# Attention probabilities times values behind the interleaved jobs instead of ahead of them, in a gated cross-attention and feed-forward kernel

## The reference

```
q = rope((layernorm(x) @ Wq) per head)            # 32 heads of 16
k = rope((ctx @ Wk) per head);  v = ctx @ Wv
w = softmax(q k^T / 4)                            # per batch and head, 256 x 256
x = x + tanh(g_xattn) * ((w v) @ Wout + bout)
h = square(relu(layernorm(x) @ up)) @ down + (layernorm(x) @ expert) * (sum of the 2 largest gate logits)
x = x + tanh(g_ffn) * (layernorm(h) * gamma + beta)
```

## Time and profile before

| | |
|---|---|
| median of 3 runs | 1567.08 us |
| the profiled execution | 1566.75 us, span 1564.9 us |
| TensorE, matmul busy | 1515.9 us (97% of the span) |
| TensorE, weight load busy | 1125.0 us (72%) |
| VectorE busy | 980.2 us (63%) |
| ScalarE busy | 635.0 us (41%) |
| GpSimd busy | 337.9 us (22%) |
| chain that ended last | TensorE 88%, VectorE 7%, issue 2% |
| mean granted TensorE clock | 0.986 of full speed |

### The profile page before, as it was taken

One profiled execution on the slowest core, in us unless ns is written; L12 is line 12 of the kernel. 1 busy time (PEld: TensorE's weight loads), 2 busy tenths in 40 slices (PEclk: granted clock), 3 DMA queues, 4 the chain that ended last, 5 costly groups with the idle time before them and its releaser, 6 DMA issues.

```text
span 1564.9 us, 25920 instructions
## 1 busy us (share of the span) xinstructions
PE 1515.9 (97%) x9498; PEld 1125.0 (72%) x9498; DVE 980.2 (63%) x1416; ACT 635.0 (41%) x962; POOL 337.9 (22%) x406
## 2 busy tenths in 40 slices
PE   7789999999999999979999999999999999999997
PEld 6556666666666666646787888878888888788886
DVE  7788888888888888755655436435354264453524
ACT  4365665655555666665432222222222222222221
POOL 5323233333333333112101002001020020110202
PEclk9699999999999999999999999999999999999999
DMA  6645555555555555544411001101011010010101
GB/s 174 142 98 141 134 137 138 131 142 139 135 135 143 127 127 136 121 134 120 147 61 35 27 21 47 35 15 47 21 35 47 1 54 27 22 40 21 55 0 41
DMA packets 80623, 131.11 MB, mean 84 GB/s; under 512 B 21624, under 2 KB 35064, under 8 KB 80504
## 3 DMA queue, kind: packets, MB, share of 16 engines
q1 hardware_dynamic: 80504, 129.48, 32.4%
HBM read 51.17 MB, written 16.78 MB: 43 GB/s over the span
## 4 chain that ended last, share of the span: by engine, by line
PE 88%; DVE 7%; issue 2%; POOL 1%; ACT 1%; DMA 0%; SPq 0%; POOLq 0%; DVEq 0%; ACTq 0%
PE pP L1113 17%; PE pT L1113 11%; PE pA L1314 11%; PE pO L1113 11%; PE pB L1314 11%; PE pA L1211 7%; PE pO L1239 7%; PE pB L1227 3%; PE pM L1113 3%; DVE mneg L1534 3%; PE pP L1120 2%; PE pM L1120 2%; PE pT L1195 1%; PE pM L1281 1%; PE pM L1187 1%
## 5 line engine op out<-in xcount | busy, mean ns | idle before, releaser
L1534 DVE TENSOR_REDUCE mneg<-pA 128x4 f32<-128x1024 f32 x250 | 305.7, 1223 | 97.7 <-PE pA L1211 93.2
L1012 ACT ACTIVATE probs<-pB 128x1024 f32<-128x1024 f32 x249 | 255.8, 1027 | 213.2 <-PE pB L1227 203.3
L811 POOL TENSOR_SCALAR var_eps<-meanvar 128x1 f32<-128x1 f32 x96 | 34.6, 360 | 986.1 <-DVE meanvar L1416 985.9
L1637 DVE TENSOR_TENSOR relu<-relu 128x512 f32<-128x512 f32 x128 | 88.4, 690 | 252.3 <-ACT hid L1066 252.3
L1314 PE MATMUL pA<-dn,hid 128*128 128x512 f32 x768 | 197.1, 392 | 1.7 <-DVE hid L1639 1.5
L1314 PE MATMUL pB<-dn,hid 128*128 128x512 f32 x768 | 195.0, 389 | 0.0
L1113 PE MATMUL pP<-fT,up 128*128 128x512 f32 x768 | 188.5, 394 | 0.0
L1113 PE MATMUL pO<-fT,up 128*128 128x512 f32 x768 | 184.7, 389 | 0.0
L1314 PEld LDWEIGHTS pA<-dn,hid 128*128 128x128 f32 x768 | 142.9, 188 | 34.4 <-DVE hid L1639 5.1
L1113 PEld LDWEIGHTS pO<-fT,up 128*128 128x128 f32 x768 | 144.0, 188 | 30.3 <-issue 0.4
L1314 PEld LDWEIGHTS pB<-dn,hid 128*128 128x128 f32 x768 | 144.1, 188 | 30.0
(11 more groups left out here) (200 smaller groups left out, 1989.8 us busy)
## 6 DMA issues: line engine op xcount, KB each, us to landing
stk<-kT SPq DMA_DIRECT2D x180, 128.0 KB, 2.9
stq<-qT SPq DMA_DIRECT2D x180, 128.0 KB, 2.9
fres<-x_scratch SPq DMA_DIRECT2D x34, 256.0 KB, 2.9
xin<-x SPq DMA_DIRECT2D x32, 256.0 KB, 2.9
numer<-av_s SPq DMA_DIRECT2D x128, 64.0 KB, 2.4
xres<-x SPq DMA_DIRECT2D x32, 256.0 KB, 2.9
x_scratch<-xres SPq DMA_DIRECT2D x32, 256.0 KB, 2.4
out<-y_s SPq DMA_DIRECT2D x32, 256.0 KB, 2.0
```

Of the source, the lines that this page charges most:

```text
L811: nc.gpsimd.tensor_scalar_add(var_eps[:], meanvar[:, 1:2], EPS).then_inc(ve_made, 1)
L1012: nc.scalar.activation(probs[:, s % 4, :, :, :].rearrange("p a b s -> p a (b s)"), psum[:, :, :], ACT.Exp).then_inc(exp_done, 1)
L1534: nc.vector.tensor_reduce(mneg[par][:, :, 2 * u:2 * u + 2].rearrange("p t q -> p q t"), psum[:, :, :].rearrange("p q (t k) -> p q t k", t= ...
L1637: nc.vector.tensor_tensor(r[:], r[:], r[:], ALU.mult).then_inc(sq_made, 1)
```

## The change

In TensorE's step, the loop over the jobs moves ahead of the product:

```diff
@@ -1260,12 +1260,12 @@
                     if within(i):
                         logits_b(i, par % 2, s)
+                    for name in names_at(i, s):
+                        job(name, i, par)
                     if s in VALUES and within(i):
                         times_v(i, par % 2, VALUES[s])
                     elif s == 0 and within(i - 1):
                         times_v(i - 1, (par + 1) % 2, GROUPS - 1)
-                    for name in names_at(i, s):
-                        job(name, i, par)
                     if planned(tile_at, i, s) is not None:
                         turned(0, planned(tile_at, i, s))
```

## The result

| | us | ratio to before, 95% interval |
|---|---|---|
| before, median of 4 runs beside it | 1567.06 | |
| changed, median of 4 runs (1586.88 to 1589.35) | 1587.12 | 1.013 [1.0113, 1.0148] |
| changed, profiled execution | 1586.89, span 1585.1 | |

The change costs 20.1 us. The forecast was 1586, from 1580 to 1594. All of it arises in the attention loop: the kT1 of iteration 13 starts at 653.93 instead of 633.92, 20.0 us late, and the first matmuls of the feed-forward gate (L1281) start at 748.37 instead of 728.02, 20.35 us late, against 20.2 us in the span.

The account below looks back on a forecast made before the run. It took TensorE's stream in the attention loop as the limit, busy 41.91 of 42.06 us an iteration. Losses of 13.7 us at step 9 and 5.5 at steps 5 to 7 gave 1586, range 1580 to 1594.

Parts of the forecast that it names:

- The work on TensorE: Attention loop: same matmuls with new neighbours leave no hole, 0 us, with 0.01 us either way for each of 7 steps.
- Step 9: kT1 loses the product that covered its wait for GpSimd's sum: 0.98 us in each of 14 iterations, 13.7 us.
- Steps 5 to 7: ScalarE stands at pO, so step 6's exp and b(7) come late: 0.39 us, 14 times, 5.5 us.
- The sum: Whole kernel: 13.7 + 5.5 = 19.2 us more, 1586.3 us against the median of 1567.08.
- The other steps: Steps 0, 10, 12, 14: ScalarE's lateness covered by six-matmul jobs, 0 us; X0 in step 0 pays 0 to 0.02 us.
- Only step 9: Rival: only step 9 is paid, ScalarE's pile-up in step 6 finds slack; 1580.8 us, chance 0.16.
- More jobs late: Rival: X0, X1, V0 or b(14) also arrive ahead of their input, 3 to 8 us; 1589 to 1594, chance 0.13.
- The clock: Rival: TensorE's waits of about 1.1 us lower its clock, 1.7 us an iteration, 24 us; 1610, chance 0.05.
- Cheaper neighbours: Rival: product beside logits is cheaper, so each of 7 steps gains; 12 us faster, 1555, chance 0.03.
- No change: Rival: waits at kT1 and b(7) are absorbed because the rotation chain comes earlier; 1567, chance 0.03.

Follow-up runs that it names:

- e8: Changed kernel, with K1's and Q1's rotations ahead of maxima(8) and maxima(9), and step 5's pO copy behind those of kT0 and X1: 1566.13 us, ratio 0.9996.
- e1: Kernel before, with the new order (jobs, then product) in step 9 alone: 1581.39 us, ratio 1.0097.
- e2: Kernel before, with the new order (jobs, then product) in step 5 alone: 1572.53 us, ratio 1.0037.
- e5: Changed kernel, with ScalarE's copy of step 5's pO put behind the copies of kT0 and X1: 1581.75 us, ratio 1.0106.
- e3: Kernel before, with the new order in steps 0, 2, 10, 12 and 14 only: 1572.66 us, ratio 1.0038.
- e4: Changed kernel, with K1's two rotation products ahead of maxima(8) on VectorE: 1579.16 us, ratio 1.0081.
- e9: Kernel before, old order, with K1's rotation ahead of maxima(8), kT0 moved from step 5 to 6, K1 using pT: 1564.05 us, ratio 0.9984.

## Why the prediction was right, point by point

**The work on TensorE: 0.** Right, and shown twice: steps 0, 2, 12 and 14 keep their length to within 0.02 us in the changed kernel, in the median of the iterations (for instance step 14, 3.25 before and 3.26 after), and e8 has the new order at no cost. The Trainium skill ("TensorEngine Tiling (Array Packing)", Key Properties) has a drain at each change of mode; the runs agree in that the same number of changes costs the same, in whichever order; what one change costs, none of them shows alone.

**Step 9, 0.98 us.** Right to the hundredth: the step takes 3.31 us where it took 2.33, 14 times, 13.7 us. e1 has it with 14.3, of which the 0.09 us of its step 10 are some 1.3.

**Steps 5 to 7, 0.39 us.** The mechanism was right, the size too small: the step to b(7) grew by 0.40 (0.34 to 0.74 after a(7)), as worked out, but K1 then comes 0.43 us after b(7) instead of 0.33. Together 0.50 to 0.51 us, 7 us in 14 instead of 5.5. The sum ended at b(7)'s start and put what follows it at nothing. It is not the wait as such that costs the 0.1 us. In iteration 15 of the kernel before, a group of logits that stands by itself is followed after 0.43 us too, with no wait ahead of it, and the a at 94.00, behind a wait of 1.09 us, by its b after the usual 0.34. TensorE's timeline of the kernel before, that b and the group by itself:

```profile
94.34 0.40 PE L1227 MATMUL pB<-stq,stk 50*128 50x256 f32 x4
...
715.39 0.50 PE L1227 MATMUL pB<-stq,stk 50*128 50x256 f32 x4
715.82 1.06 PE L1239 MATMUL pO<-probs,v 128*17 128x256 f32 x16
```

So b(7) costs 0.33 us directly behind a(7) and 0.43 once the late exp has parted them; the price could have been read before the change. e2 and e5 show the 0.5 us put in and taken out.

**The sum.** 14 x (0.98 + 0.51) = 20.9 against a growth of 1.48 x 14 = 20.7 and a whole of 20.1. The forecast of 19.2 was 1 us low, for the 0.1 us behind b(7) that it lacked.

**The other steps: 0.** Right for the changed kernel, and for a reason that the prediction had only in part. It looked for the nearest input at X0 (0.02 us paid, as bounded, but 0.38 once, in iteration 1) and X1. That one was late in one of the 12 iterations, where step 5 took 2.87 us instead of 2.69; it came 0.06 us after VectorE had read the last result in the same PSUM tile, pP (336.92 to 336.98), and its own input was not the last to come. What it left out was O0< in step 10, which would come 0.2 us before VectorE has freed pT. Nothing of that is seen in the changed kernel, because the wait at kT1 gives VectorE a whole microsecond. That this term came out at 0 was therefore luck: the prediction followed when inputs are ready, and not when the PSUM tile that a job writes into comes free. e3 and e4 have the wait, and both of those expectations were wrong mainly for this reason.

**Rivals.** Only step 9 (1581): e1's time, and out by e2. More jobs late (1589 to 1594): true of single places (X0 and X1 once each, O0< in e3 and e4), but not of this mix. The clock (1610): the granted clock of the iteration stayed at 1.00, with a wait of about 1.02 us in each. Cheaper neighbours (1555): out by e8. No change: out.

## What to carry to other kernels

An instruction that stands ahead of one whose input is late is cover, and moving it costs its own length, up to the wait. Before moving one, write down for each step when the next instruction's input is there, when the tile that it writes into is free, and when the engines that follow take the result; where two streams take results in another order than the first makes them, the later engine stands. And a cost found for one place alone doesn't add up with others: a wait hides the next one, so taking the first away shows the second (1.1 us an iteration expected, 0.75 found).

## What was not expected of the hardware

- A group of logits parted from its neighbour is followed by the next group after 0.43 us, and one directly behind another after 0.33 (b(7) after and before the change; 715.39 without any wait).
- A transpose job costs 0.58 us alone between other shapes (e9), and two side by side 1.03.
- Waits of 1.02 us in every iteration left the granted clock at 1.00 (262.29 to 305.81). A wait of 1.09 us and one of 0.39 shortly behind it were followed by 0.68 in e8's iteration 1, and nearly the same two, 1.09 and 0.38, left it at 1.00 in the changed kernel (104 to 110). What decides between them is open.
